# Moving two kinds of transpose from the edge of an attention quarter to the middle of it

## The reference

```python
xn = _layernorm(x)
q, k, v = xn @ Wq.T, xn @ Wk.T, xn @ Wv.T
scores = jnp.einsum('bsqhd,bthd->bqhst', qh, kh) * scale
probs = jax.nn.softmax(scores, axis=-1)
a_dot = jnp.einsum('bqhst,bthd->bsqhd', probs, vh)
out = a_dot * (1.0 - w) + a_mem * w          # a_mem: elu(q) @ memory, normalised
x = x + out + moe(xn)                        # 8 experts, the best 2 of each token, and a shared one
```

## Time and profile before

| | us |
|---|---|
| three runs, median | 790.97 |
| three runs, lowest and highest | 789.17, 791.29 |
| the profiled execution, its own time | 790.88 |
| its span, first to last instruction | 789.1 |
| granted TensorE clock, mean over the span | 0.994 |

### The profile page before, as it was taken

How to read it: one execution, slowest core, us unless ns; L and a number is a source line. 1 busy time by engine, 2 the same in 40 slices (tenths; PEclk the granted TensorE clock), 3 DMA queues, 4 the chain that set the end, 5 groups by cost and what they waited for, 6 DMA issues and landing times.

```text
span 789.1 us, 14228 instructions
## 1 busy us (share of the span) xinstructions
PE 713.8 (90%) x3976; PEld 373.1 (47%) x3977; DVE 582.3 (74%) x800; ACT 486.8 (62%) x886; POOL 132.3 (17%) x282
## 2 busy tenths in 40 slices
PE   4999999799898898988999888889999999998997
PEld 2455445422222222222222122668777877787887
DVE  5375488799999999999999872666776667665754
ACT  1472600388888888888888886656565555545431
POOL 1000000756531111111111110000000000004740
PEclk9999999899999999999999999999999999999999
DMA  9629100177310011111001460041111111122431
GB/s 315 234 66 329 35 0 1 59 245 237 94 59 23 24 32 32 31 31 31 22 25 31 145 214 14 28 147 53 40 53 45 48 45 48 49 79 80 126 102 40
DMA packets 49950, 65.35 MB, mean 83 GB/s; under 512 B 8168, under 2 KB 42880, under 8 KB 49920
## 3 DMA queue, kind: packets, MB, share of 16 engines
q1 hardware_dynamic: 38848, 40.85, 16.5%
q10 hardware_dynamic: 8000, 15.73, 5.9%
q0 software_dynamic: 3072, 8.39, 3.4%
HBM read 40.15 MB, written 24.38 MB: 82 GB/s over the span
## 4 chain that ended last, share of the span: by engine, by line
PE 66%; ACT 11%; issue 10%; DVE 7%; DVEq 2%; POOL 1%; ACTq 1%; DMA 1%; SPq 1%; POOLq 0%
PE ps L1355 13%; PE ps L1384 11%; PE ps L1408 9%; ACT att L729 8%; PE ps L1236 7%; PE ps L1486 6%; PE ps L1454 5%; DVE smax L991 4%; PE ps L1228 3%; PE ps L1501 3%; ACT att_r L709 2%; PE ps L1196 2%; PE ps L1261 2%; PE ps L1344 1%; DVEq L1041 1%
## 5 line engine op out<-in xcount | busy, mean ns | idle before, releaser
L991 DVE TENSOR_REDUCE smax<-ps 128x2 f32<-128x1024 f32 x256 | 302.5, 1221 | 37.3 <-PE ps L1261 34.3
L729 ACT ACTIVATE att<-ps 128x512 f32<-128x512 f32 x512 | 267.7, 604 | 55.6 <-PE ps L1408 52.9
L1408 PE MATMUL ps<-att 51*128 51x512 bf16 x512 | 166.4, 386 | 32.9 <-ACT att L729 16.3
L1261 PE MATMUL ps<-att 48*128 48x512 bf16 x512 | 164.0, 387 | 1.4 <-DVE smax L991 1.4
L1355 PE MATMUL ps<-att,v_head 128*32 128x512 f32 x1024 | 137.5, 609 | 1.7 <-ACT o_sb L688 0.6
L1408 PEld LDWEIGHTS ps<-att 51*128 51x128 bf16 x512 | 39.7, 93 | 202.2 <-ACT att L729 95.9
L1048 DVE TENSOR_TENSOR att_r<-big,att_r 128x1024 fp32r<-128x1024 f32 x76 | 89.8, 1222 | 60.3 <-ACT att_r L709 60.3
L1384 PE MATMUL ps<-att_r 128*128 128x512 f32 x456 | 115.7, 402 | 15.3 <-DVE att_r L1052 13.8
L1384 PEld LDWEIGHTS ps<-att_r 128*128 128x128 f32 x456 | 84.1, 188 | 39.3 <-issue 19.3
L709 ACT ACTIVATE att_r<-big 128x1024 fp32r x74 | 74.4, 1053 | 19.7 <-issue 17.6
L1454 PE MATMUL ps<-big,xn 128*128 x312 | 73.7, 380 | 0.0
(11 more groups left out here) (164 smaller groups left out, 691.7 us busy)
## 6 DMA issues: line engine op xcount, KB each, us to landing
big<-w ACTq DMA_DIRECT2D x8, 1024.0 KB
q_stacks<-big SPq DMA_DIRECT2D x12, 512.0 KB
att<-q_stacks SPq DMA_DIRECT2D x64, 96.0 KB
slot_x<-zeros SPq DMA_DIRECT2D x1, 4992.0 KB, 17.1
e_x<-slot_x SPq DMA_DIRECT2D x39, 128.0 KB, 2.0
slot_y<-xn SPq DMA_DIRECT2D x39, 128.0 KB, 1.7
big<-w ACTq DMA_DIRECT2D x8, 512.0 KB
att<-k_stacks SPq DMA_DIRECT2D x64, 48.0 KB
```

What stands on the lines that cost most here:

```text
L729: act.activation(probs[:, t % 2, g, :], ps[:, RING[turn_of(u) % 3], :], ACT.Exp, scale=SCALE)\
L991: dve.reduce_max(smax[:, s % 2, :].rearrange("p (half v) -> p half v", half=2)[:, :, v], ps[:, bank:bank + 2, :], X_AXIS).then_inc(max_don ...
L1261: return pe.matmul(ps[:, bank + half, :], q_st[s][rows, g, P * st:P * (st + 1)], k_st[s][rows, :], start=True, stop=True)
L1408: pe.matmul(ps[:, RING[turn % 3], :], k_st[s][rows, P * t:P * (t + 1)], q_st[s][rows, g, :], start=True, stop=True).then_inc(scores_ready, 1)
```

## The change

`MAX_AT` goes from 4 to 6 and `OUT_AT` from 13 to 11. On PE the turned maxima now come behind unit 5, between the two pairs of quarter 1, and the output transposes behind unit 9, between the two pairs of quarter 2. On ACT `negate_max` moves from ahead of exponential 4 to ahead of exponential 6, and `copy_oT` from ahead of exponential 12 to ahead of exponential 10; `evacuate_o` stays ahead of exponential 5. The guests' banks change from 5 and 5 to 4 and 7. No instruction is added or taken away, and no other number of the schedule changes.

```diff
-        TURNS, MAX_AT, OUT_AT = 18, 4, 13
+        TURNS, MAX_AT, OUT_AT = 18, 6, 11
@@ exps (ACT)
-                    if u == 4 and not last:
+                    if u == MAX_AT and not last:
                         negate_max(i + 1, s + 1, blk * 2 + (s + 1) // 2)
...
-                        if u == 12:
+                        if u == OUT_AT - 1:
                             copy_oT(blk * 2 + (s // 2 - 1), (s // 2 + 1) % 2)
@@ step (PE)
                                 if half == 1:
                                     ins.then_inc(a_ready, 1)
-                    if t == OUT_AT // G - 1 and s % 2 == 0 and not first:
-                        transpose_o(pair - 1, (s // 2 + 1) % 2)
+
+                        if v == MAX_AT // 2 - 1 and not last:
+                            transpose_max(i + 1, s + 1)
+                        if v == (OUT_AT - 1) // 2 - 1 and s % 2 == 0 and not first:
+                            transpose_o(pair - 1, (s // 2 + 1) % 2)
 
                     if t > 0:
                         weighted_values(i, s, t - 1, pair)
                     elif not first:
                         weighted_values(i - 1, s + 3, ST - 1)
-                    if t == MAX_AT // G - 1 and not last:
-                        transpose_max(i + 1, s + 1)
-
```

## The result

The changed kernel takes 806.77 us (median of four, 804.53 to 808.78), the kernel before 790.51. The ratio is 1.0205, 95% interval 1.018 to 1.023: 16.3 us slower, where 19 was forecast (810.1, range 804.5 to 816). The profiled execution took 807.78 us, with a span of 806.0.

The account below looks back on a forecast made before the run. A chain of first score, its exponential, last score and burst was taken to bound each quarter. 790.88 + 15.6 (loop) + 4.2 (written-out steps) - 0.6 (step 0) = 810.1 us, range 804.5 to 816.

Parts of the forecast that it names:

- The bound: In each attention quarter, a chain of first score, its exponential, last score and burst: 2.47 us, 2.96 with a guest.
- second link: In a quarter's chain, exponential to last score: with a guest, the fourth score waits for the second exponential, 0.49 us more.
- The loop: Steps 4 to 27, twelve pairs: 1.30 us more a pair, +15.6 us.
- first link: In a quarter's chain, first score's start to its exponential's start: 0.50 us in the loop, 0.08 shorter in written-out steps.
- The written-out steps: Steps 1 to 3 and 28 to 31: even ones +0.21, odd ones +0.85, step 31 +0.98, together +4.2 us.
- Step 0: First attention step: burst 1.1 us earlier after L1313, empty turn in quarter 2 costs 0.49; net -0.6 us.
- the rival: In step 0 the clock stays up: another 1.3 to 2 us less, 808.5 us in all; chance 0.18.
- The sum: Whole kernel: 790.88 + 15.6 + 4.2 - 0.6 = 810.1 us.
- within three: Whole kernel: measured time within three us of the forecast 810.1; chance 0.62.
- The move that pays: Whole kernel: the fourth score's wait is no limit, so 14.0 us faster, 777; chance 0.08, including coming out even.
- VectorE as a second limit: Loop: VectorE's later reductions add 0.1 us in 64 quarters, 6 us, so 816; chance 0.08.
- The clock in the loop: Rival: a third of the loop's 96 quarters fall to 1.2 GHz, 39 us more, so 849; chance 0.04.

Follow-up runs that it names:

- the empty turn at the edge: The changed kernel, but odd steps and step 0 count their empty output turn at 13, a quarter's edge, not at 11; 797.38 us, ratio 1.0081.
- the swap: The kernel before, with ACT's two waits ahead of a quarter's first exponential swapped, the burst's first, the score's second; 787.86 us, ratio 0.9965.
- the short guest: The changed kernel, with the four f32 output transposes replaced by one bf16 matmul and the attention's outputs left out; 807.29 us, ratio 1.022.
- the kernel with the copy later: The changed kernel, with the copy L688 (evacuate_o) behind exponential 5, not ahead of it; 803.15 us, ratio 1.0179.

## Why the prediction was right, point by point

**The bound.** Right. The chain of first score, exponential, last score and burst holds the quarters that the change touches: it gave 2.47 and 2.96 to 0.01, the first quarter of an odd step stayed at 2.78 as forecast, and moving its second link by one exponential and back moved the time both ways, without any matmul, exponential or copy moved (the empty turn).

**The loop.** 1.14 a pair against 1.30, so 13.7 us against 15.6. The step that was mis-sized is the first link, which I took as 0.50 throughout. It is 0.42 in quarter 1, where the score's wait stands on the exponential itself (308.72 to 309.14 above); in the other quarters of the loop it stands on a register instruction ahead, as the swap shows. That is 0.07 and 0.08 in the two quarters 1 of a pair, all of the difference. The row that tells it was there: the bursts of the written-out steps were 0.08 shorter, and I read that as a matter of the loop, not of the waits' place.

**The written-out steps.** 4.0 against 4.2. The prediction let odd steps pay 0.36 in quarter 1 as in the loop; there it was 2.88 for 2.56, 0.32.

**Step 0.** Wrong in sign. L1313 to burst did shorten, from 2.06 to 1.20 (0.94 was forecast), and the empty turn cost 0.48 (4.18 for 3.70), but the granted clock stayed low for longer. The profiled execution, in the three stretches from L1313 to the burst of quarter 3:

```profile
151.13:152.33 1.20, 1.20 (x5) 0.24 (x6) 0.32 (x1) 0.59 (x2) 1.04 (x2) 0.50 0.00 0
152.33:156.51 4.18, 3.92 (x18) 0.54 (x16) 2.43 (x2) 2.23 (x5) 3.17 (x4) 0.50 0.28 97
156.51:160.22 3.71, 3.71 (x19) 0.60 (x17) 1.98 (x3) 1.90 (x5) 0.97 (x1) 0.50 0.20 71
```

Together 9.09 us at 1.2 GHz, for 8.41 before, in which the clock was back for part of the last quarter: +0.7 for -0.6. What the same code takes when the clock stays up, the profiled execution of the short guest shows, whose step 0 is that of the changed kernel:

```profile
150.45 0.24 PE L1313 MATMUL ps<-eye,max_parts 128*48 128x128 bf16 x1 [1.10 <-POOL max_parts L535]
...
151.15 1.06 PE L1353 MATMUL ps<-att,v_head 128*32 128x512 f32 x8
...
154.03 1.06 PE L1353 MATMUL ps<-att,v_head 128*32 128x512 f32 x8
...
156.43 1.06 PE L1353 MATMUL ps<-att,v_head 128*32 128x512 f32 x8
```

That is 5.98 us, with the granted clock at 1.00 throughout, and the kernel with the copy later, also unchanged in step 0, has 5.99. So the low clock costs 3.1 us here, and a step 0 with the clock up comes out 1.8 under the 7.8 of the forecast; the rival said 1.3 to 2. The idle time of PE just ahead of L1313 doesn't tell the two apart: 1.10 and 1.20 us where the clock stayed up, 1.19 where it fell.

Between executions it varies: the four of the changed kernel had mean clocks of 0.999, 0.995, 0.993 and 0.991 and took 804.5, 805.8, 807.8 and 808.8 us, in that order. The two profiled executions with the clock up in step 0 also had 0.999, so by the mean clock that rival came about in one of four, and its 3.1 us can be most of the spread of 4.2. Only the 807.8 was profiled, and why the clock falls in some executions stays open.

**The sum.** Span against span it is +16.9. The loop gives +13.7, the written-out steps +4.0, step 0 +0.7; a DMA issue on ACT (L735) that took 1.30 us delayed the first exponential of step 2, +0.6; a like place in step 28 gave 0.24 back; and the stretches before and behind, which the change doesn't touch, were 1.9 shorter in this execution. 13.7 + 4.0 + 0.7 + 0.6 - 0.2 - 1.9 = 16.9. The forecast's total was 2.3 too high against this execution: 1.9 too much in the loop and 0.2 in the written-out steps, 1.3 too little in step 0, and the rest (1.5) is what the change does not touch. The errors of the loop and of step 0 partly cancel, which is luck. Against the median, 806.77, the total was 3.3 too high: inside the range, 0.3 outside the "within three" that had the chance of 0.62.

**The rivals.** The move that pays is out: the changed kernel is slower, and the empty turn at the edge and the short guest show why. VectorE as a second limit is out: its waits for maxima rose from 34.3 to 43.4 us, and the quarters with a guest take the chain's 2.96. The clock in the loop stayed at 1.00 in the changed kernel, with 38 us of PE idle in 246. By that rule of the Trainium skill (TensorE: Matmul & The Clock Gate, A second HAM failure mode: psum-queue depth-cycling) the time would have swung with the clock, and no trace here shows it in the loop; the one long fall near the end of the attention is told below.

## What to carry to other kernels

In a ring of few buffers, count for the *last* taker of a burst whose release it waits for; a guest in the middle of the burst moves that by one, and costs one step of the engine that frees the buffers (0.49 us, one exponential, here) even where its own work is hidden, and even where the turn stays empty. Put unused turns at an edge, where nobody waits for them. And before moving work out of an edge, ask whether the edge or the ring sets the pace: here 0.59 us of transposes were truly on the path in even steps, and moving only those won 5 us.

## What the runs showed of the hardware

- From a score's start to its exponential's it took 0.42 us where the score's semaphore stood on the exponential, and 0.50 where it stood on a register instruction ahead of it and the exponential carried the other wait (314.12 - 313.70 with ACT's waits swapped, 317.16 - 316.66 in the earlier trace rows). In the written-out code it was a semaphore instruction ahead, and the quarter took 2.45 for 2.39. Two swapped lines made 3 us in 790.
- VectorE's reductions of 128 x 1024 from PSUM take 1.22 us each but overlap a little when queued: six took 7.14 us with ACT's waits swapped and 7.22 before, so they start 1.18 to 1.20 apart on average, and two fit into a quarter of 2.39.
- The granted clock can fall late and for long. In the profiled execution of the kernel with the turned maxima moved alone it stood at 0.50 through quarters 2 and 3 of step 30 and the first of step 31, where the changed kernel had 1.00 from 490.75 to 506.44:

```profile
485.85:497.99 12.14, 11.36 (x42) 2.00 (x41) 0.68 (x3) 6.35 (x14) 1.34 (x2) 0.50 0.01 2
```

From 475.09 to 485.85 PE had been busy in 8.91 of 10.76 us. From the burst at 482.26 to the one at 512.81 it took 30.55 us; the same seven quarters of the changed kernel took 23.37, so this fall costs some 7 us. Three of the six executions of that kernel lie some 11.5 us above the other three and have the lower mean clocks; none of the four of the changed one does. Only one of the three was profiled, and its step 0 had the low clock too. What tips it is open.
